# Attention and routing on one core: sums of five blocks on GpSimd, last halves routed in denser order

## The reference, cut to what matters

```python
# x (4, 1024, 256) gives the queries and 1024 of the keys
# ctx (4, 77, 192), mask; H = 4 heads of 64
ln, xn = layernorm(layernorm(x)) * g + b, layernorm(ctx) * g2 + b2
q = ln @ Wq.T
k, v = split(concat([xn @ Wkv.T, ln @ Wlkv.T], axis=1))       # 77 + 1024 keys
attn = softmax(where(mask, rmsnorm(q) * s @ rmsnorm(k).T, -max))
x = x + (attn @ v) @ Wo.T + bo                                # residual
h = layernorm(x)                                              # 4096 tokens
scores = sigmoid(h @ gate_w.T); sfc = scores + bias           # 64 experts in 8 groups
# best 4 groups by the sum of their best two, best 8 experts in them, weights normed, x 2.5
# every expert takes its first 256 tokens in token order:
y = (silu(buf @ w_gate) * (buf @ w_up)) @ w_down
x = x + sum over a token's slots of y * weight
```

## Time and profile before

| | us |
|---|---|
| median of three runs | 1167.11 |
| the profiled execution | 1164.94 |
| its span, first to last instruction | 1163.0 |
| TensorE busy | 945.4 (81%) |
| VectorE busy | 616.8 (53%) |
| GpSimd busy | 587.2 (50%) |
| ScalarE busy | 461.3 (40%) |
| stretch 770.7 to 848 (77.3): TensorE, VectorE, GpSimd busy | 12.2, 36.5, 53.4 |
| stretch 848 to 1163 (315): TensorE, VectorE, GpSimd busy | 215.7, 83.5, 205.1 |

### The profile page before, as it was taken

The page is one execution under the profiler, slowest core; times in us unless marked ns, Lnnn a source line. Parts: engine busy times, 40 slices in busy tenths (PEclk is TensorE's granted clock), DMA queues, the critical chain, the costliest instruction groups (busy, mean ns, idle before and its releaser), DMA issues.

```text
span 1163.0 us, 12926 instructions
## 1 busy us (share of the span) xinstructions
PE 945.4 (81%) x3736; PEld 598.3 (51%) x3736; DVE 616.8 (53%) x1898; ACT 461.3 (40%) x930; POOL 587.2 (50%) x530
## 2 busy tenths in 40 slices
PE   3779999999999999999999999961079977878700
PEld 1445565645655554555555545531068866666500
DVE  4473536896568776467857666647124323332300
ACT  3633665733856444566453432530023322222100
POOL 3620042307616625722853737276736667777782
PEclk9878999999999998999999998985579988998955
DMA  8519301113202323300124403015069987877668
GB/s 304 213 41 386 138 1 39 37 44 144 70 1 78 124 68 100 108 1 7 68 73 165 165 19 116 20 48 222 8 193 295 258 185 135 145 140 136 82 68 153
DMA packets 79285, 133.66 MB, mean 115 GB/s; under 512 B 13419, under 2 KB 48027, under 8 KB 79217
## 3 DMA queue, kind: packets, MB, share of 16 engines
q1 hardware_dynamic: 47345, 91.04, 23.9%
q0 software_dynamic: 31872, 41.80, 18.4%
HBM read 60.76 MB, written 93.00 MB: 132 GB/s over the span
## 4 chain that ended last, share of the span: by engine, by line
PE 57%; POOL 11%; issue 10%; DMA 9%; DVE 7%; ACT 4%; POOLq 0%; DVEq 0%; ACTq 0%; SPq 0%
PE ps_o L1158 22%; PE ps_u L1074 7%; PE ps_s L1142 6%; PE ps_s L1144 5%; DMA out_rows<-again,row_ids 5%; PE ps_u L1097 4%; POOL out_rows L1023 4%; POOL odd_sum L1023 3%; DMA odd_sum<-again,row_ids 3%; POOL slot_rows L956 3%; PE ps_u L1167 2%; PE ps_u L1085 2%; PE ps_u L1113 2%; PE ps_u L1124 1%; ACT den L1365 1%
## 5 line engine op out<-in xcount | busy, mean ns | idle before, releaser
L956 POOL DMA_INDIRECT slot_rows<-rows,slot_idx x256 | 251.7, 983 | 212.2 <-issue 182.7
L1474 DVE TENSOR_REDUCE mp<-ps_u 128x1 f32<-128x512 f32 x256 | 164.7, 686 | 107.4 <-PE ps_u L1097 105.7
L1348 ACT ACTIVATE probs<-ps_s 128x512 f32<-128x512 f32 x256 | 139.5, 596 | 160.0 <-PE ps_s L1144 158.5
L1158 PE MATMUL ps_o<-probs,V 128*128 128x512 f32 (+1 forms) x288 | 141.1, 614 | 2.9 <-ACT den L1365 2.9
L1158 PE MATMUL ps_o<-probs,pool 128*128 128x512 f32 (+1 forms) x288 | 140.5, 611 | 3.2 <-ACT den L1365 3.2
L971 POOL TENSOR_TENSOR pool<-pool,rs_y 128x1024 f32<-128x1024 f32 (+1 forms) x20 | 32.9, 1647 | 198.9 <-DVEq L1469 198.7
L1219 PE MATMUL ps_u<-again 128*128 128x256 f32 x512 | 130.1, 400 | 0.0
L1617 DVE TENSOR_SCALAR again<-ps_o,again 128x256 f32<-128x256 f32 x128 | 56.1, 480 | 138.8 <-DMA out_rows<-again,row_ids 79.1
L1023 POOL DMA_INDIRECT out_rows<-again,row_ids x64 | 99.2, 1550 | 53.4 <-DVE row_ids L1618 20.8
L1023 POOL DMA_INDIRECT odd_sum<-again,row_ids x64 | 99.1, 1549 | 37.0 <-issue 17.7
L1144 PE MATMUL ps_s<-qbT,Kb 65*128 65x512 f32 (+1 forms) x288 | 117.2, 407 | 0.0
(11 more groups left out here) (181 smaller groups left out, 1443.7 us busy)
## 6 DMA issues: line engine op xcount, KB each, us to landing
again<-in_wexp SPq DMA_DIRECT2D x64, 384.0 KB, 6.5
slot_rows<-rows SPq DMA_DIRECT2D x2, 10272.0 KB, 33.1
again<-slot_rows SPq DMA_DIRECT2D x64, 321.0 KB, 4.2
Kb<-K SPq DMA_DIRECT2D x16, 275.5 KB, 3.9
odd_sum<-rows SPq DMA_DIRECT2D x1, 4352.0 KB, 22.4
pool<-in_x SPq DMA_DIRECT2D x4, 1024.0 KB, 5.6
xres<-in_x SPq DMA_DIRECT2D x8, 512.0 KB, 3.8
out_rows<-xres SPq DMA_DIRECT2D x8, 512.0 KB, 3.0
```

Source lines behind the costliest of these rows:

```text
L956: pool.indirect_dma_start(out=slot_rows, out_offset=bass.IndirectOffsetOnAxis(ap=slot_idx[x][:, q, k:k + 1], axis=0), in_=rows[x][:, q, :] ...
L1158: i = pe.matmul(ps_o[:, hh, :], V[b % 2][0:rk, pr, kt, DH * hh:DH * hh + P], probs[0:rk, n % NPR, hh, :], start=(kt == 0), stop=(kt == NKT ...
L1348: act.activation(probs[:, n % NPR, hh, :], ps_s[:, u % NSC, :], ACT.Exp).then_inc(s["probs_made"], 1)
L1474: v.tensor_reduce(mp[:, i, tile, half:half + 1], bank((*t, i))[:, :], AX.X, ALU.max).then_inc(s["emptied_vec"], 1)
```

## The change

Three things in one. (1) In five blocks, (0,0,0), (0,1,1), (1,0,1), (1,1,1) and (2,0,1), the values product has 64 columns a head, and both heads write the two halves of one bank, the blocks alternating between two banks; GpSimd adds the nine tiles of probabilities of both heads into `acc` (eight additions a block), and one product per head with a matrix of ones (`sums`) spreads the total over partitions. (2) The routing tasks of (2,1) and (3,0) are put four to a slot, not two. (3) The last half's rows are normed in two pairs of tiles, the choice of tile 0 ahead of the store and of the second pair's end. Small things: the mask row is bf16, the gain table has one head's width, the logits share a tile with the scores.

```diff
+NORMED = {(B - 1, 1): ((0, 2), (2, 4))}
+CHOSEN = {}
...
+        "scat": {"pool": 1.3}, "scale": {"dve": 2.3}, "lag": {}, "acc": {"dve": 1.4}, "acc_pool": {"pool": 2.5},
+        "sums": {"pe": 1.05, "act": 0.6}}
 SCORES, VALUES, COPIES = {"pe": 0.95, "act": 1.2}, {"pe": 1.75}, {"act": 2.4}
+VALUES_SUMMED, COPIES_SUMMED = {"pe": 1.05}, {"act": 0.6}
...
+SUMMED = {(0, 0, 0): range(1, NKT), (0, 1, 1): range(1, NKT), (1, 0, 1): range(1, NKT), (1, 1, 1): range(1, NKT), (2, 0, 1): range(1, NKT)}
...
-        for q in range(2):
-            self.add("scale", *order[-1], q)
...
-        for t in self.route_tasks(B - 1, 1, parts=[(q, q + 1) for q in range(QT)]):
+        rows_made = [self.row_tasks(B - 1, 1, *tiles) for tiles in NORMED[(B - 1, 1)]]
+        chosen = [[(kind, B - 1, 1, q, q + 1) for kind in CHOICE] + [("scat", B - 1, 1, q, k) for k in range(TOPK)]
+                  for q in range(QT)]
+        for t in ([("scale", *order[-1], 0)] + rows_made[0] + [("scale", *order[-1], 1)] + chosen[0] + rows_made[1]
+                  + [("store", B - 1, 1)] + chosen[1] + chosen[2] + chosen[3]):
             self.add(*t)
...
-                self.slots.setdefault(first + n // 2, []).append(t)
-            first += len(tasks) // 2
+                self.slots.setdefault(first + n // 4, []).append(t)
+            first += len(tasks) // 4
...
+                elif kind == "acc_pool":
+                    b, x, pr, kt = t[1:]
+                    n = step_no[t[1:]]
+                    rk = rows_of(kt)
+                    pool.wait_ge(s["probs_made"], 2 * n + 2)
+                    if kt == 1:
+                        before = sum(block_no[u[1:]] < block_no[(b, x, pr)] for u in sums_units)
+                        if before:
+                            wait_full(pool, sums_units[before - 1])
+                        pool.tensor_tensor(acc[:], probs[:, (n - 1) % NPR], probs[:, n % NPR], ALU.add
+                                           ).then_inc(s["probs_summed"], 1)
+                    else:
+                        pool.wait_ge(s["probs_summed"], summed[t[1:]] - 1)
+                        pool.tensor_tensor(acc[0:rk], acc[0:rk], probs[0:rk, n % NPR], ALU.add
+                                           ).then_inc(s["probs_summed"], 1)
...
-                    pe.matmul(dst.rearrange("p (q k) -> p q k", q=QT), one_row[:],
+                    pe.matmul(dst.rearrange("p (q k) -> p q k", q=QT), ones[0:1, :],
...
+                        if (b, x, pr) in SUMMED:
+                            i = pe.matmul(ps_o[DH * hh:DH * (hh + 1), o_bank[(b, x, pr)], :],
+                                          V[b % 2][0:rk, pr, kt, 2 * DH * hh:DH * (2 * hh + 1)],
+                                          probs[0:rk, n % NPR, hh, :], start=(kt == 0), stop=(kt == NKT - 1),
+                                          skip_group_check=True)
...
+                elif kind == "sums":
+                    b, x, pr = t[1:]
+                    pe.wait_ge(s["probs_summed"], summed[(*t[1:], NKT - 1)])
+                    for hh in range(2):
+                        i = pe.matmul(bank(t)[DH * hh:DH * (hh + 1), :], V[b % 2][:, pr, 0, DH:2 * DH], acc[:, hh, :],
+                                      start=True, stop=True, skip_group_check=True)
+                    i.then_inc(s["unit_full"], 1)
...
                         act.wait_ge(s["values_done"], n - NPR + 1)
+                        if steps[n - NPR] in summed:
+                            act.wait_ge(s["probs_summed"], summed[steps[n - NPR]])
...
+                    if t[1:] in SUMMED:
+                        i = act.activation(oT[:, pr, :], ps_o[:, o_bank[t[1:]], :], ACT.Copy)
...
+                elif kind == "sums":
+                    wait_full(act, t)
+                    act.activation(den[:], bank(t), ACT.Copy).then_inc(s["emptied_act"], 1)
```

176 lines of the change are left out of this document (117 added, 59 removed).

## The result

The changed kernel took 1177.42 us (median of 4 runs, 1176.80 to 1181.01), the kernel before 1164.32 (4 runs, 1158.56 to 1170.71): a ratio of 1.0122, interval 1.0081 to 1.0164. The forecast was 1140, range 1118 to 1167. The change made the kernel slower by just over the 1% that can be told from none, on the other side of the forecast.

The account below looks back on a forecast made before the run. TensorE was taken to bound attention and GpSimd the routing tail. Attention -17.4 and tail -9.5 make -26.9 us: 1138.0 from the profiled execution's 1164.9, which lies 2.2 under the median, so 1140, range 1118 to 1167.

Parts of the forecast that it names:

- TensorE's term: Values product in five attention blocks: a pair of heads takes 1.05 us, not 1.72; net -24.9 us with the sums product.
- everything overlaps: Rival: values pair at 0.86 us and no holding of VectorE, the whole at 1119 us; chance 0.17.
- saves nothing: Rival: the half-width values pair gains nothing, +8.6 us in attention, tail -9.5, the whole at 1166 us; chance 0.10.
- Length of an addition: GpSimd's additions of probabilities in the summed blocks: 2.4 us each, between 1.9 and 2.6, keeping pace with the shortened step.
- Held VectorE time: VectorE instructions stretch beside GpSimd's additions: 0.35 us per us of addition, 27 us over 32 additions, 6.7 a block.
- What held time costs: Two of four later summed blocks overshoot by 15.2 us; half reaches the end, leaving -12.4 there and -17.4 in attention.
- The tail: Routing after attention: earlier scatters and tile 0 of (3,1) ready sooner bring the experts forward, -9.5 us, ends -14 and -2.
- The closer packing: Packing routing of (2,1) and (3,0) puts more VectorE work into single steps: counted 0, ends -3 and +3 us.
- VectorE is held for the whole of each addition: Slower rival: held above 33.9 us, four blocks grow; at the full 2.4 us per addition, 1195 us; chance 0.10.
- The tail gives little: Rival: the hole follows the weight loads and GpSimd waits for the first tile, -2 us, whole at 1148; chance 0.15.
- The signs named: Wrong if pair stays 1.7 us, additions exceed 2.6, TensorE waits at L1253 for sums, or (0,1,1), (1,1,1) grow over 3.

Follow-up runs that it names:

- e11: The changed kernel with no block summed, the closer packing, row split and small edits kept: 1151.90 us, 0.991 of the kernel before.
- e12: The changed kernel with 35 of GpSimd's 40 additions cut to 8 of 512 columns a head: 1130.60 us, 0.975 of the kernel before.
- e9: The changed kernel with no block summed and routing tasks packed two to a half step again, row split kept: 1158.16 us, 0.995 of the kernel before.
- e16: The changed kernel with 35 of GpSimd's 40 additions cut to 256 of 512 columns a head: 1154.30 us, 0.993 of the kernel before.
- e6: The changed kernel with only block (2,0,1) summed, packing kept: 1154.53 us, 0.991 of the kernel before.
- e5: The changed kernel with all 40 additions done by VectorE, none by GpSimd: 1163.26 us, 0.999 of the kernel before.
- e7: The changed kernel summing only (0,0,0) and (0,0,1) with GpSimd's additions and (3,1,1) with VectorE's: 1152.61 us, 0.993 of the kernel before.
- e15: The changed kernel with only block (0,0,0) summed, packing kept: 1143.08 us, 0.983 of the kernel before.

## Why the prediction was wrong

**TensorE's term: right.** Pair 1.01 us for 1.05; net on attention with most of the holding gone, e11 to e12, -19.8 us for -24.9. Five additions of e12 are still whole; what else the missing 5 us are is not shown. The rivals "everything overlaps" and "saves nothing" both fall by the 1.01.

**Length of an addition: right**, 2.38 us and 2.47 for the first of a block, for 2.4.

**Held VectorE time: a little small.** 0.35 us per us of GpSimd was taken. From e12 to the changed kernel GpSimd adds 75.4 us (83.3 - 7.9) and VectorE's busy time grows by 34.2 on the whole page (628.9 to 663.1): 0.45. For 32 additions that is 35 us instead of 27.

**What held time costs: this step failed.** The prediction compared VectorE's busy time of a block plus 6.7 with the block's length, found an overshoot in two of four blocks, and let "half of the 15.2 reach the end". With 0.45 put in (8.6 us a block), the same rule finds an overshoot in three blocks and lets 10.4 us reach the end, in place of 7.6. The runs show 45.0 us for 35.3 us held, 1.3 each. Two things were missing.
- *Room on average is not room in order.* VectorE had 15 us free in (2,0,1), and TensorE still idled 12.5. The held instructions are those of the routing's chain, the maxima stand behind them in VectorE's fixed order, and TensorE's three side banks are full meanwhile. Of the 45.0 us, 19.7 are such idle time.
- *The clock.* No term of the prediction had it. The other 25.3 us are TensorE busy longer with the same instructions, 83 us of them at 1.2 GHz where e12 has 31: 0.77, 0.88, 0.66 and 0.86 granted in the four blocks that had 1.00.

**The tail: right in size, wrong in its parts.** -9.5 forecast, 392.3 - 382.8 = 9.5 measured. But of the changed kernel's rows, to be read against the earlier trace rows (GpSimd's timeline, then SyncE's),

```profile
771.82 0.99 POOL L1018 DMA_INDIRECT slot_rows<-rows,slot_idx  x1 [16.06 <-issue]
...
806.52 0.98 POOL L1018 DMA_INDIRECT slot_rows<-rows,slot_idx  x1 [0.30 <-issue]
814.28 0.98 POOL L1018 DMA_INDIRECT slot_rows<-rows,slot_idx  x1 [6.78 <-issue]
...
857.06 0.98 POOL L1018 DMA_INDIRECT slot_rows<-rows,slot_idx  x1 [1.96 <-issue]
```

```profile
863.09 3.69 SPq L963 DMA_DIRECT2D again<-slot_rows  x8
```

the first load of the experts comes 70.6 us after attention's end, 6.8 sooner than before's 77.4, and the experts themselves took 2.7 us less (314.9 to 312.2), which was not priced. (3,0)'s scatters gained 8.5 us on the end of attention (20.7 for 12.2), not 13, the hole grew by 1.8 (5.02 to 6.78), and that makes the 6.8. GpSimd is never seen waiting for tile 0, whose rows were done at 813.05 and its first scatter ran at 819.41: GpSimd still sets the end, as before, and not tile 0, from whose readiness the prediction counted. The closer packing, counted 0 within 3, gave more than half of what packing and split gave together (e9, e11). That the sum came out at 9.5 is luck.

**The rivals.** "VectorE is held for the whole of each addition" ended on the right side with too high a price (1195) for a holding that was not whole (0.45, not 1). By its rule the four blocks stay no longer than before up to 33.9 us held, and 35 us would have given a kernel near 1154 (1167.1 + 1.1 - 14.5); the kernel was 13 us slower than before. The room that it counted is not there: of the dose runs, e16 has 13.7 us held more than e12 and is 19.8 us behind it in attention. "The tail gives little" did not come about.

**The signs named.** One of those that would make the forecast wrong came, in both its blocks: (0,1,1) and (1,1,1) grew by 4.9 and 5.7 us, more than 3. Pair and additions came out as named. L1611 did stretch, to 2.12 us in (1,0,1) and 0.71 to 0.92 in the other three; L1680 runs once in each of the four, for 0.42, 2.17, 0.42 and 2.17, and its mean over attention is the same 0.92 in e11. TensorE idled 2.7 us in all before L1253, none of it for the sums; these stand late in the order, up to 11 us after the block, and ScalarE waits 4.6 us for them in all. The last copy out of ps_o stood at 792.5, not 753, and the first load of the experts at 863.1, not 821.

What stays open: by stretches of 6 us, TensorE had the lower clock for some 27 us in (1,1,1) behind a wait of 1.5, and for some 17 in (0,1,1). There the clock fell at 232.3, ahead of the wait of 7.1 us and just behind one of 1.84 for ScalarE's probabilities; ScalarE had itself waited 3.72 us for VectorE, whose L634, of eight columns, had been held to 2.33 us. No run varied a wait or the clock alone. Nor was it tried which two summed blocks hurt each other: (2,0,1) alone (e6) takes no longer than unsummed, among five it takes ten us more.

## What to carry to other kernels

Before giving a second engine work that reads and writes the same memory as the first, look in the trace for instructions of the first that end together with those of the second, and price their holding by the chain behind them, not by average busy share: here 1.3 us for each us held, and about as much in e5 for VectorE's own work in the same place. Where the tuned engine is TensorE, cut its stretches by granted clock as well as by waits, since a small wait can be followed by a long stretch at half speed (1.5 us and 27 here) that busy times and waits do not show. To test such a cause, shorten the suspected instructions in two doses and leave the order alone. And follow a gain from block to block, in blocks that were not touched as well: e7 and e15 got or lost most of theirs there.
